# Opening of a four-layer kernel: loads in pieces in the order of use, scratch rows zeroed later

## The chip, the cores and the metric

The kernel runs on one core of one Trainium2 chip. Its time is the device time of one execution in microseconds; the median of several executions counts, and a change is measured by the ratio of the medians.

## The reference

x is (8, 256, 256), the context (8, 256, 192), the mask (8, 256) with one flag for each context row. Four layers follow one another, each a cross attention or a similarity and then a feed-forward part; LayerNorm stands before each.

```python
x = x + L0_xattn(layernorm(x), ctx, mask, ...)   # masked cross attention, 16 heads of 16
x = x + L0_ffn(layernorm(x), ...)                # top-1 experts, rows scattered to slots
x = x + L1_xattn(layernorm(x), ctx, ...)         # cosine similarity
x = x + L1_ffn(layernorm(x), ...)                # local transformer
x = x + L2_xattn(layernorm(x), ctx, ...)         # cross attention with biases and a scale
x = x + L2_ffn(layernorm(x), ...)                # top-2 experts
x = x + L3_xattn(layernorm(x), ctx, ...)         # cross attention, output bias
x = x + L3_ffn(layernorm(x), ...)                # grouped experts

def L0_xattn(x, context, context_mask, Wq, Wk, Wv, Wo):
    q, k, v = heads(x @ Wq), heads(context @ Wk), heads(context @ Wv)
    scores = einsum('bhid,bhjd->bhij', q, k) * 16 ** -0.5
    scores = where(context_mask[:, None, None, :], scores, -finfo.max)
    return merge(einsum('bhij,bhjd->bhid', softmax(scores), v)) @ Wo
```

## The kernel before

Five engines run their own instruction streams and meet at semaphores: TensorE (PE), VectorE (DVE), ScalarE (ACT), GpSimd (POOL) and SyncE (SP), which issues most DMAs. The 2048 rows of x stay on the chip as 16 tiles of 128 rows (`c.x`), the context transposed (`c.ctxT`, two chunks of 128 partitions by 2048 columns). A phase is a block: all engines leave it together.

`load_phase` is the first block. SP issues the loads of x (2 MB), the context (2 MB) and the identity, then, when GpSimd has filled a tile with zeros, one store that zeroes all 5120 slot rows of the scratch `rows_in` (5 MB), and waits for the loads. VectorE raises 72 semaphores to their starting count, one instruction each (line 143).

`xattn_phase` is the cross attention of layers 0, 2 and 3 (the tags L0x, L2x and L3x). SP issues its weights, and for layer 0 the mask, all on one semaphore (lines 364 to 373). VectorE measures mean and variance of the first four tiles (`measure(0)`), GpSimd takes the power -0.5 of the variance (line 351), and VectorE then waits for all loads, turns the mask into two things (line 779 to 782: `anyk`, whether a sequence has any key, and `mbias`, one row of 2048 biases), scales wq, and goes to `normalise_rows(0)`. TensorE begins when every load is in and VectorE's steps are done:

```python
            pe.wait_ge(*loaded(16 * n_loads))
            pe.wait_ge(*mstep(MSTEPS))
            project_keys(0)
            turn_rows(0)
            project_queries(0)
```

`project_keys(b)` (line 452) multiplies the context of sequence b with wk. ACT and DVE split the result into a leading part and a rest (`lead_keys`, `rest_keys`, line 795 or 798); `turn_rows(b)` (line 442) waits for that rest and for the normalised rows and transposes them, and `project_queries(b)` follows. Keys and queries go through DRAM to be stacked in three parts: `send_keys`, `stack_keys`, `send_queries`, `stack_queries` on SP, an order written out by hand, each waiting for the one before to land. Then TensorE goes over 8 sequences of 16 heads: scores of the next sequence for its row maxima (taken by DVE, line 816), and scores of this one with the maxima put in as a row. The maxima make a round trip through DRAM on ACT's own queue (`send_maxima`, `top_queries`, lines 654 and 661), twice a sequence. In the loop over sequences SP sends the queries of b + 2 and the keys of b + 3.

In `dispatch_phase` of layer 0's experts GpSimd waits for the zeros and scatters rows into `rows_in` (line 1097).

## Time and profile before

| | |
|---|---|
| median of 3 runs | 2955.56 us (2951.53 to 2962.20) |
| the profiled execution | 2948.41 us, its span 2946.5 us |
| mean granted clock of TensorE | 0.879 |
| busy | PE 2322.9 us, DVE 1290.0, ACT 1063.6, POOL 616.9 |
| DMA over the whole run | 165.65 MB |

The span runs from the first to the last instruction. Times in the rows are microseconds from the span's start; a shape is partitions x elements; SPq, ACTq and the like are the queues of an engine, where issues and waits stand. "idle before" names what ended the idle time of the engine just before the instruction. The granted clock is 1.00 at 2.4 GHz and 0.50 at 1.2 GHz.

### The profile page before, as it was taken

The numbers are of one execution on the slowest core, as the hardware profiler recorded it, in microseconds if no ns is written. First come the engines' busy times: TensorE is split into PE (matmuls) and PEld (weight loads), VectorE is DVE, ScalarE is ACT, GpSimd is POOL, SyncE is SP. The second block draws the span as 40 slices with busy tenths as digits, with TensorE's granted clock in tenths as the row PEclk, the third lists the DMA queues.
The fourth block names the chain that finished last, engine by engine and source line by source line (L and its number), as shares of the span: only waits on it lengthen the run. The fifth ranks groups of instructions, "written<-read, shape, count | busy, mean of one in ns | idle before, by whom it ended". The sixth has DMA issues, their size and how long they took to land. (4 is left out here: it accounts for less than half of the span.)

```text
span 2946.5 us, 43378 instructions
## 1 busy us (share of the span) xinstructions
PE 2322.9 (79%) x13240; PEld 1675.6 (57%) x13241; DVE 1290.0 (44%) x2837; ACT 1063.6 (36%) x2491; POOL 616.9 (21%) x623
## 2 busy tenths in 40 slices
PE   2896298448799698889597897897999179838998
PEld 1564197224465474456375564467999156517887
DVE  3564200459665425956522564300000246465554
ACT  0464132214355422346531355213444035513332
POOL 0001200217521323722131000220000400023333
PEclk9798599669799798979797699898999569969999
DMA  6660332000000100000101672213220366200001
GB/s 197 116 119 12 128 130 87 27 26 0 10 0 3 44 1 26 0 10 0 47 1 35 116 123 37 77 53 125 79 110 18 88 119 123 43 13 27 22 21 34
DMA packets 119273, 165.65 MB, mean 56 GB/s; under 512 B 14394, under 2 KB 106269, under 8 KB 114045
## 3 DMA queue, kind: packets, MB, share of 16 engines
q1 hardware_dynamic: 113236, 150.64, 20.5%
q0 software_dynamic: 4608, 12.59, 1.3%
q10 hardware_dynamic: 1320, 1.03, 0.2%
q8 instruction: 61, 1.00, 0.2%
q14 instruction: 48, 0.39, 0.0%
HBM read 114.43 MB, written 47.32 MB: 55 GB/s over the span
## 5 line engine op out<-in xcount | busy, mean ns | idle before, releaser
L816 DVE TENSOR_REDUCE xa_mx<-ps 128x2 f32<-128x512 f32 x384 | 256.9, 690 | 221.3 <-PE ps L478 213.0
L668 ACT ACTIVATE xn_tok<-ps 128x512 f32<-128x512 f32 x384 | 227.4, 602 | 168.0 <-PE ps L486 166.4
L478 PE MATMUL ps<-xa_ks,xa_qs 48*128 48x256 f32 (+1 forms) x768 | 182.5, 349 | 47.6 <-DVE xa_mx L816 21.0
L1315 PE MATMUL ps<-ex_tiles,ex_w 128*128 x1792 | 213.2, 278 | 7.7 <-issue 4.2
L1315 PEld LDWEIGHTS ps<-ex_tiles,ex_w 128*128 128x128 f32 x1792 | 212.6, 195 | 11.3 <-issue 8.5
L1321 PE MATMUL ps<-ex_w,ex_h 128*128 128x256 f32 x896 | 202.7, 379 | 0.0
L478 PEld LDWEIGHTS ps<-xa_ks,xa_qs 48*128 48x128 f32 (+1 forms) x768 | 118.5, 208 | 137.5 <-issue 80.9
L1835 PE MATMUL ps<-lp_wqkv,lp_hs 128*128 128x512 f32 x384 | 176.4, 611 | 4.6 <-ACT lp_hs L1879 4.3
L1321 PEld LDWEIGHTS ps<-ex_w,ex_h 128*128 128x128 f32 x896 | 166.0, 190 | 20.2
L486 PE MATMUL ps<-xa_qs,xa_ks 49*128 49x256 f32 (+1 forms) x768 | 173.3, 332 | 0.7 <-ACT xn_tok L668 0.7
L1335 ACT ACTIVATE ex_h<-ps,ex_b 128x128 f32<-128x128 f32 x296 | 108.8, 368 | 152.8 <-PE ps L1315 132.7
L452 PE MATMUL ps<-ctx_T,xa_wk 128*128 128x256 f32 x192 | 59.7, 464 | 128.4 <-DVE xa_wq L789 102.9
L255 PE MATMUL ps<-ident,ln_row 128*128 128x128 f32 x192 | 46.9, 399 | 122.9 <-DVE ln_row L225 121.5
L1373 POOL DMA_INDIRECT xn_tok<-rows_out,rows_back x32 | 31.5, 984 | 530.7 <-DMA rows_out<-ex_tiles 521.5
L1351 DVE TENSOR_TENSOR ex_tiles<-ps,ex_b 128x256 f32 x37 | 15.7, 425 | 276.6 <-PE ps L1321 270.0
L232 POOL TENSOR_TENSOR ln_rstd<-ln_var,pow_half 128x16 f32<-128x16 f32 x7 | 20.4, 2913 | 497.7 <-DVE ln_var L214 497.7
L1835 PEld LDWEIGHTS ps<-lp_wqkv,lp_hs 128*128 128x128 f32 x384 | 72.2, 194 | 90.1 <-issue 85.3
L1622 POOL TENSOR_TENSOR ge_hl<-ge_h,ge_hh 128x512 fp32r<-128x512 f32 x64 | 82.6, 1291 | 195.0 <-ACT ge_hh L1611 195.0
L452 PEld LDWEIGHTS ps<-ctx_T,xa_wk 128*128 128x128 f32 x192 | 41.9, 230 | 140.7 <-DMA xa_bo<-in_L3x_bo_dram 59.9
L486 PEld LDWEIGHTS ps<-xa_qs,xa_ks 49*128 49x128 f32 (+1 forms) x768 | 111.3, 195 | 9.3 <-ACT xn_tok L668 6.8
L1533 PE MATMUL ps<-ge_xh,ge_wh 128*128 128x512 f32 x256 | 81.8, 401 | 40.7 <-PEq L1400 24.5
L2085 ACT ACTIVATE lw_p<-ps,lw_nm 128x128 f32<-128x128 f32 (+1 forms) x256 | 106.3, 425 | 14.6 <-DVE lw_nm L2136 14.6
...
## 6 DMA issues: line engine op xcount, KB each, us to landing
...
x_keys<-xa_khl SPq DMA_DIRECT2D x24, 512.0 KB, 5.9
x_queries<-xa_qhl SPq DMA_DIRECT2D x24, 512.0 KB, 2.9
di_rows<-rows_in SPq DMA_DIRECT2D x16, 512.0 KB, 3.8
...
```

What stands on the lines that cost most here:

```text
L452: ins = nc.tensor.matmul(c.ps[:, W_BANK, ch * S:(ch + 1) * S], wk[:, k, ch * P:(ch + 1) * P], c.ctxT[:, k, b * S:(b + 1) * S], start=(k == ...
L478: ins = nc.tensor.matmul(c.ps[:, M_BANK + h % 2, qt * S:(qt + 1) * S], qs[r:r + ROWS_M, b % Q_BUFS, n, qt * P:(qt + 1) * P], ks[r:r + ROWS ...
L486: ins = nc.tensor.matmul(c.ps[:, S_BANK + (HEADS * b + n) % 3, kt * S:(kt + 1) * S], ks[r:r + ROWS_S, b % K_BUFS, h // 2, kt * P:(kt + 1) ...
L668: nc.scalar.activation(pT[:, h % SLOTS].rearrange("p k q -> p (k q)"), c.ps[:, S_BANK + (HEADS * b + n) % 3], ACT.Exp).then_inc(exped.sem, 1)
L816: nc.vector.tensor_reduce(mx[:, half, :, col], c.ps[:, M_BANK + h % 2].rearrange("p (t n) -> p t n", t=2), AX_X, ALU.max).then_inc(max_put ...
L1315: ins = nc.tensor.matmul(c.ps[:, f % 4, 0:P], w1[:, par, k, f * P:(f + 1) * P], tile_of(n)[:, k], start=(k == 0), stop=(k == KD - 1))
L1321: ins = nc.tensor.matmul(c.ps[:, 4, 0:D], h[:, f], w2[:, par, f], start=(f == 0), stop=(f == FC - 1))
L1335: nc.scalar.activation(h[:, f], c.ps[:, f % 4, 0:P], ACT.Relu if first else ACT.Silu, bias=0.0 if first else b1[:, par, f:f + 1]).then_inc ...
L1533: ins = nc.tensor.matmul(c.ps[:, 2 * (g % 2) + m, :], wp[:, par, at:at + I3], xp[:, k, cols], start=(a == 0 and k == 0), stop=(a == 2 and ...
L1622: nc.gpsimd.tensor_tensor(hl[:, g % 2], h[:, g % 2], hh[:, g % 2].bitcast(F32), ALU.subtract).then_inc(h_rest.sem, 1)
L1835: ins = nc.tensor.matmul(c.ps[:, 3 * tt + n, :], hs[:, k, tt * P:(tt + 1) * P], wqkv[:, k, n * INNER:(n + 1) * INNER], start=(k == 0), sto ...
L2085: ins = nc.scalar.activation(pr[:, h % AHEAD, lo:hi], c.ps[:, 1 + h % AHEAD, lo:hi], ACT.Exp, bias=nm[:, h, n:n + 1], accum_out=rs[:, h, n ...
```

## The change

The first block loses its loads, the store of zeros and the wait for them; what is left of it is raising the semaphores, now dealt to VectorE, TensorE, ScalarE and GpSimd (three names more), and GpSimd's four small memsets. The attention block issues, for layer 0: wk, the mask, the first 512 columns of the context, the first four tiles of x, the identity, wq, the other tiles of x, wv, the rest of the context, wo. Each has a semaphore of its own except wv and wo. TensorE begins with wk and the first context part; it waits for the scaled wq only ahead of `project_queries(0)`, and for wv and wo at head 4 of the first pass. The two mask operations that make `mbias` go from VectorE to GpSimd, ahead of its power steps, and read the bytes of one partition; `anyk` stays on VectorE, straight from the bytes. wq is scaled after `normalise_rows(0)` instead of before it. SP waits for `mbias` after `send_keys(0)`. The zeros are stored in eight pieces of 640 KB, one at the end of each turn of SP's loop over sequences; GpSimd's wait ahead of the scatter counts all eight. Layers 2 and 3 get the same waits, in the order wk, wq (with its scale), wv, wo, bo. `CTX_PARTS` is ((0, 512), (512, 2048)), `GROUPS` ((0, 4), (4, 16)); `mask_in`, `ctx_in`, `x_in`, `ident_in`, `kw_in` and `qw_in` are the new DMA semaphores, `any_key`, `rows_masked` and `scaled` the new ones of the engines.

```diff
@@ -134,33 +134,34 @@
 
 def load_phase(c):
 
-    nc, loaded, set_up = c.nc, c.sig("loaded"), c.sig("set_up")
+    nc, set_up = c.nc, c.sig("set_up")
     with nc.Block() as block:
+        def raise_signals(eng, quarter):
+            for name in SIGNALS[quarter::4]:
+                if name != "set_up":
+                    eng.sem_inc(c.sig(name).sem, START)
+
         @block.vector
         def _(dve):
-            for name in SIGNALS:
-                if name != "set_up":
-                    dve.sem_inc(c.sig(name).sem, START)
-
-        @block.sync
-        def _(sp):
-            for name, dst in (("x", c.x), ("ctxT", c.ctxT), ("ident", c.ident)):
-                sp.dma_start(dst[:], c.dram[name]).then_inc(loaded.sem, 16)
-
-            sp.wait_ge(*set_up(4))
-            rows = c.dram["rows_in"][0:SLOT_ROWS].rearrange("(a p) d -> p a d", p=P)
-            sp.dma_start(rows, c.zero[:].to_broadcast([P, SLOT_ROWS // P, D])).then_inc(c.sig("scratch_zeroed").sem, 16)
-            sp.wait_ge(*loaded(48))
+            raise_signals(dve, 0)
+
+        @block.tensor
+        def _(pe):
+            raise_signals(pe, 1)
+
+        @block.scalar
+        def _(act):
+            raise_signals(act, 2)
 
         @block.gpsimd
         def _(pool):
+            raise_signals(pool, 3)
             nc.gpsimd.memset(c.ones[:], 1.0).then_inc(set_up.sem, 1)
             nc.gpsimd.memset(c.half[:, 0], 0.5).then_inc(set_up.sem, 1)
             nc.gpsimd.memset(c.half[:, 1], -0.5).then_inc(set_up.sem, 1)
             nc.gpsimd.memset(c.zero[:], 0.0).then_inc(set_up.sem, 1)
             pool.sem_inc(set_up.sem, START)
             pool.wait_ge(*set_up(4))
-    loaded.spent(48)
     set_up.spent(4)
 
 
...
@@ -346,6 +351,14 @@
             nc.gpsimd.memset(consts[:, 0], -1.0).then_inc(consts_set.sem, 1)
             nc.gpsimd.memset(mx[:], 0.0)
             nc.gpsimd.memset(va[:], 1.0).then_inc(mstep.sem, 1)
+            if masked:
+                pool.wait_ge(*mask_in(16))
+                nc.gpsimd.tensor_scalar(mask[:], mask8[0:1], -1.0, HUGE, ALU.add, ALU.mult).then_inc(rows_masked.sem, 1)
+                pool.wait_ge(*rows_masked(1))
+                pool.wait_ge(*any_key(1))
+                nc.gpsimd.tensor_tensor(
+                    mbias[:].rearrange("p (b s) -> p b s", b=B), mask[:].rearrange("p (b s) -> p b s", b=B),
+                    anyk[0:1].unsqueeze(2).to_broadcast([1, B, S]), ALU.mult).then_inc(rows_masked.sem, 1)
             for n, (lo, hi) in enumerate(GROUPS):
                 pool.wait_ge(*variance(n + 1))
                 nc.gpsimd.tensor_tensor(rstd[:, lo:hi], var[:, lo:hi], c.half[:, 1, lo:hi], ALU.pow
...
@@ -359,18 +372,33 @@
                 pool.wait_ge(*bias_added(B))
             pool.wait_ge(*powered(len(GROUPS)))
             pool.wait_ge(*mstep(1))
+            if masked:
+                pool.wait_ge(*rows_masked(2))
 
         @block.sync
         def _(sp):
-            for dst, name in ((wk, "wk"), (wq, "wq"), (wv, "wv"), (wo, "wo")):
-                sp.dma_start(dst[:], dram[tag + name]).then_inc(loaded.sem, 16)
+            sp.dma_start(wk[:], dram[tag + "wk"]).then_inc(kw_in.sem, 16)
+            if masked:
+                sp.dma_start(mask8[:], dram["mask"].partition_broadcast(P)).then_inc(mask_in.sem, 16)
+                lo, hi = CTX_PARTS[0]
+                sp.dma_start(c.ctxT[:, :, lo:hi], dram["ctxT"][:, :, lo:hi]).then_inc(ctx_in[0].sem, 16)
+                lo, hi = GROUPS[0]
+                sp.dma_start(c.x[:, lo:hi], dram["x"][:, lo:hi]).then_inc(x_in[0].sem, 16)
+                sp.dma_start(c.ident[:], dram["ident"]).then_inc(ident_in.sem, 16)
+            sp.dma_start(wq[:], dram[tag + "wq"]).then_inc(qw_in.sem, 16)
+            if scale_in:
+                sp.dma_start(qcol[:], dram[tag + "qcol"]).then_inc(qw_in.sem, 16)
+                sp.dma_start(qscale[:], dram[tag + "scale"].partition_broadcast(P)).then_inc(qw_in.sem, 16)
+            if masked:
+                lo, hi = GROUPS[1]
+                sp.dma_start(c.x[:, lo:hi], dram["x"][:, lo:hi]).then_inc(x_in[1].sem, 16)
+            sp.dma_start(wv[:], dram[tag + "wv"]).then_inc(loaded.sem, 16)
+            if masked:
+                lo, hi = CTX_PARTS[1]
+                sp.dma_start(c.ctxT[:, :, lo:hi], dram["ctxT"][:, :, lo:hi]).then_inc(ctx_in[1].sem, 16)
+            sp.dma_start(wo[:], dram[tag + "wo"]).then_inc(loaded.sem, 16)
             if biased:
                 sp.dma_start(bo[:], dram[tag + "bo"].partition_broadcast(P)).then_inc(loaded.sem, 16)
-            if scale_in:
-                sp.dma_start(qcol[:], dram[tag + "qcol"]).then_inc(loaded.sem, 16)
-                sp.dma_start(qscale[:], dram[tag + "scale"].partition_broadcast(P)).then_inc(loaded.sem, 16)
-            if masked:
-                sp.dma_start(mask8[:], dram["mask"].partition_broadcast(P)).then_inc(loaded.sem, 16)
 
             def send_keys(b):
                 sp.wait_ge(*k_rest(b + 1))
...
@@ -421,6 +449,9 @@
             stack_queries(1)
             send_keys(2)
             stack_keys(2)
+            if masked:
+                clear = SLOT_ROWS // P // B
+                rows = dram["rows_in"][0:SLOT_ROWS].rearrange("(a p) d -> p a d", p=P)
             for b in range(B):
                 if b + 2 < B:
                     send_queries(b + 2)
...
@@ -428,10 +459,15 @@
                 if b + 3 < B:
                     send_keys(b + 3)
                     stack_keys(b + 3)
+                if masked:
+                    sp.dma_start(rows[:, b * clear:(b + 1) * clear], c.zero[:].to_broadcast([P, clear, D])
+                                 ).then_inc(c.sig("scratch_zeroed").sem, 16)
 
         @block.tensor
         def _(pe):
             def turn_rows(b):
+                if masked and b == 0:
+                    pe.wait_ge(*ident_in(16))
                 pe.wait_ge(*normed(b + 1))
                 if b < 3:
                     pe.wait_ge(*k_rest(b + 1))
...
@@ -447,6 +483,8 @@
                 pe.wait_ge(*q_rest(b))
                 if b == 2:
                     pe.wait_ge(*v_put(1))
+                    if masked:
+                        pe.wait_ge(*ctx_in[1](16))
                 for ch in range(KD):
                     for k in range(KD):
                         ins = nc.tensor.matmul(c.ps[:, W_BANK, ch * S:(ch + 1) * S], wk[:, k, ch * P:(ch + 1) * P],
...
@@ -556,10 +594,12 @@
                                                wo[:, k], start=(k == 0), stop=(k == KD - 1))
                 ins.then_inc(y_done.sem, 1)
 
-            pe.wait_ge(*loaded(16 * n_loads))
-            pe.wait_ge(*mstep(MSTEPS))
+            pe.wait_ge(*kw_in(16))
+            if masked:
+                pe.wait_ge(*ctx_in[0](16))
             project_keys(0)
             turn_rows(0)
+            pe.wait_ge(*scaled(SCALES))
             project_queries(0)
             project_keys(1)
             turn_rows(1)
...
@@ -568,6 +608,7 @@
             for n in range(HEADS):
                 step(-1, n)
                 if n == 4:
+                    pe.wait_ge(*loaded(16 * n_loads))
                     project_values(0)
                 elif n == HALF:
                     turn_maxima(0, 0)
...
@@ -687,7 +728,9 @@
                 if masked:
                     act.dma_start(qs[at - 1:at].bitcast(F32).rearrange("p n g s -> p (n g) s"),
                                   consts[:, 1:2].to_broadcast([1, Q_BUFS * PAIRS, S])).then_inc(rows_set.sem, 16)
-            act.wait_ge(*mstep(MSTEPS))
+            act.wait_ge(*mstep(1))
+            if masked:
+                act.wait_ge(*any_key(1))
             lead_keys(0)
             put_rows(0)
             lead_queries(0)
...
@@ -744,6 +787,8 @@
 
             def measure(n):
                 lo, hi = GROUPS[n]
+                if masked:
+                    dve.wait_ge(*x_in[n](16))
                 for t in range(lo, hi):
                     ins = nc.vector.bn_stats(stats[:, t].rearrange("p a b -> p (a b)"), c.x[:, t])
                 chain.link(dve, ins)
...
@@ -770,24 +815,20 @@
                                                   rstd[:, n:n + 1], ALU.subtract, ALU.mult)
                 ins.then_inc(normed.sem, 1)
 
+            if masked:
+                dve.wait_ge(*mask_in(16))
+                nc.vector.tensor_reduce(anyk[:], mask8[:].rearrange("p (b s) -> p b s", b=B), AX_X, ALU.max
+                                        ).then_inc(any_key.sem, 1)
+            dve.wait_ge(*mstep(1))
             measure(0)
-            step = Steps(mstep)
-            step.n = 1
-            dve.wait_ge(*mstep(1))
-            dve.wait_ge(*loaded(16 * n_loads))
-            if masked:
-                step.link(dve, nc.vector.tensor_copy(mask[:], mask8[:]))
-                step.link(dve, nc.vector.tensor_reduce(anyk[:], mask[:].rearrange("p (b s) -> p b s", b=B), AX_X, ALU.max))
-                step.link(dve, nc.vector.tensor_scalar(mask[0:1], mask[0:1], -1.0, HUGE, ALU.add, ALU.mult))
-                step.link(dve, nc.vector.tensor_tensor(
-                    mbias[:].rearrange("p (b s) -> p b s", b=B), mask[0:1].rearrange("p (b s) -> p b s", b=B),
-                    anyk[0:1].unsqueeze(2).to_broadcast([1, B, S]), ALU.mult))
-            if scale_in:
-                step.mark(nc.vector.tensor_scalar(qcol[:], qcol[:], qscale[:, 0:1], None, ALU.mult))
-                step.link(dve, nc.vector.tensor_scalar(wq[:], wq[:], qscale[:, 0:1], None, ALU.mult))
-            else:
-                step.link(dve, nc.vector.tensor_scalar(wq[:], wq[:], scale, None, ALU.mult))
-            assert step.n == MSTEPS
+
+            def scale_queries():
+                dve.wait_ge(*qw_in(16 * n_query_loads))
+                if scale_in:
+                    nc.vector.tensor_scalar(qcol[:], qcol[:], qscale[:, 0:1], None, ALU.mult).then_inc(scaled.sem, 1)
+                    nc.vector.tensor_scalar(wq[:], wq[:], qscale[:, 0:1], None, ALU.mult).then_inc(scaled.sem, 1)
+                else:
+                    nc.vector.tensor_scalar(wq[:], wq[:], scale, None, ALU.mult).then_inc(scaled.sem, 1)
 
             def rest_keys(b):
                 dve.wait_ge(*k_put(b + 1))
...
@@ -836,6 +877,7 @@
                 nc.vector.tensor_tensor(xb, xb, c.ps[:, Y_BANK], ALU.add).then_inc(y_added.sem, 1)
 
             normalise_rows(0)
+            scale_queries()
             rest_keys(0)
             normalise_rows(1)
             rest_queries(0)
...
@@ -1091,7 +1141,7 @@
 
         @block.gpsimd
         def _(pool):
-            pool.wait_ge(*zeroed(16))
+            pool.wait_ge(*zeroed(16 * B))
             for t in range(NT):
                 for n in range(top):
                     nc.gpsimd.indirect_dma_start(c.dram["rows_in"], bass.IndirectOffsetOnAxis(slots[:, n, t:t + 1], 0),
```

## Rows read from the trace of the kernel before

**Rows 1.** Stretches: us, busy us of each engine, then granted clock, DMA share, GB/s
```profile
5.00:15.40 10.40, 0.00 (x0) 0.00 (x0) 0.00 (x0) 0.00 (x0) 0.00 (x0) 1.00 0.99 380
27.00:32.00 5.00, 0.00 (x0) 0.00 (x0) 0.00 (x0) 0.00 (x0) 0.00 (x0) 1.00 0.82 254
32.00:43.40 11.40, 0.00 (x0) 0.00 (x0) 7.45 (x6) 0.00 (x0) 0.00 (x0) 1.00 0.09 28
43.40:99.00 55.60, 38.95 (x123) 26.86 (x124) 24.50 (x52) 10.35 (x17) 2.27 (x1) 0.66 0.65 119
150.00:200.00 50.00, 47.77 (x408) 31.93 (x407) 32.50 (x57) 29.68 (x61) 0.00 (x0) 1.00 0.67 127
```

**Rows 2.** Timeline, opening: start us, us, engine, line, operation, count [idle before <-releaser]
```profile
15.42 11.40 SPq L366 DMA_DIRECT2D xa_wk<-in_L0x_wk_dram  x1
15.46 1.41 DVE L748 BATCH_NORM_STATS2 xa_stats<-x_res 128x6 f32<-128x256 f32 x4 [15.34 <-PEq L138]
...
16.38 1.80 POOL L348 MEMSET xa_v<- 128x2048 f32 x1
...
17.17 1.04 DVE L752 TENSOR_SCALAR xa_mean<-xa_total 128x4 f32<-128x4 f32 x1
...
19.29 1.02 POOL L351 TENSOR_TENSOR xa_rstd<-xa_var,pow_half 128x4 f32<-128x4 f32 x1 [1.11 <-DVE xa_var L760]
...
35.77 1.23 DVE L779 CAST xa_mask<-xa_mask 128x2048 f32<-128x2048 uint8 x1 [16.56 <-DMA xa_mask<-in_mask_dram]
37.03 2.29 DVE L780 TENSOR_REDUCE xa_anyk<-xa_mask 128x8 f32<-128x2048 f32 x1
...
42.92 0.43 DVE L789 TENSOR_SCALAR xa_wq<-xa_wq 128x512 f32<-128x512 f32 x1
43.38 0.73 DVE L769 TENSOR_SCALAR xa_row<-x_res,xa_mean,xa_rstd 128x256 f32<-128x256 f32 x2
...
43.45 3.75 PE L452 MATMUL ps<-ctx_T,xa_wk 128*128 128x256 f32 x8 [43.45 <-DVE xa_wq L789]
...
49.29 0.75 DVE L795 SCALAR_TENSOR_TENSOR xa_khl<-ps,xa_anyk,xa_khl 128x512 fp32r<-128x512 f32 x1 [5.17 <-ACT xa_khl L626]
...
50.19 0.63 PE L442 MATMUL ps<-ident,xa_row 128*128 128x128 f32 x4 [2.99 <-DVE xa_khl L795]
```

**Rows 3.** Line 143: count, ns min/median/max, first and last start us
```profile
L143 DVEq EVENT_SEMAPHORE  x72: 21/21/21, 0.8 to 7.8; - x72
```

**Rows 4.** DMA issues, first 60 us: count, KB each, us to landing
```profile
rows_in<-zero SPq DMA_DIRECT2D x1, 5120.0 KB, 30.4
...
x_keys<-xa_khl SPq DMA_DIRECT2D x1, 512.0 KB, 2.9
```

**Rows 5.** GpSimd's groups by shape: count | busy us, mean ns | idle
```profile
L1622 POOL TENSOR_TENSOR ge_hl<-ge_h,ge_hh 128x512 fp32r<-128x512 f32 x64 | 82.6, 1291 | 195.0 <-ACT ge_hh L1611 195.0
...
L1445 POOL TENSOR_TENSOR ge_xl<-xn_T,ge_xh 128x1024 fp32r<-128x1024 f32 x4 | 12.8, 3217 | 27.3 <-ACT ge_xh L1436 27.3
```

**Rows 6.** Timeline, opening of layer 3
```profile
2341.03 0.35 SPq L366 DMA_DIRECT2D xa_wk<-in_L3x_wk_dram  x1
...
2347.98 0.43 DVE L789 TENSOR_SCALAR xa_wq<-xa_wq 128x512 f32<-128x512 f32 x1 [3.41 <-DMA xa_bo<-in_L3x_bo_dram]
...
2352.83 0.69 DVE L798 TENSOR_TENSOR xa_khl<-ps,xa_khl 128x512 fp32r<-128x512 f32 x1 [3.65 <-ACT xa_khl L628]
```

**Rows 7.** Timeline, opening of layer 2, VectorE
```profile
1605.43 0.23 DVE L786 TENSOR_SCALAR xa_qcol<-xa_qcol,xa_qscale 128x2 f32<-128x2 f32 x1 [3.83 <-DMA xa_qscale<-in_L2x_scale_dram]
...
1610.61 0.69 DVE L798 TENSOR_TENSOR xa_khl<-ps,xa_khl 128x512 fp32r<-128x512 f32 x1 [3.79 <-ACT xa_khl L628]
```

**Rows 8.** Timeline of SyncE in the steady part
```profile
142.71 0.66 SPq L397 DMA_DIRECT2D xa_ks<-xa_mbias  x1
149.34 0.38 SPq L382 DMA_DIRECT2D x_queries<-xa_qhl  x1
```

**Rows 9.** Timeline of ScalarE in the steady part
```profile
147.10 0.59 ACT L638 CAST xa_qhl<-ps 128x512 fp32r<-128x512 f32 x1 [2.14 <-DMA x_maxima<-xa_mxT]
```

28 lines of the change are left out of this document (20 added, 8 removed).

## The prediction

> **What bounds the kernel now.** I read the stretches first. From 5 to 43.4 us the program does almost nothing but load: TensorE has no instruction. Up to 15.4 us 380 GB/s move, from 27 to 32 us 254, and from 32 to 43.4 us the DMA engines are idle (share 0.09) while VectorE works alone on the mask. From 150 us on TensorE is busy 47.8 of 50 us at full clock: there it sets the pace, and what is saved ahead of it moves everything behind it forward by as much [rows 1].
>
> Then the chain of starts in the opening. The first block ends when its last load has landed; the attention block's first load is issued at 15.42 us, and that one issue takes 11.40 us, because SyncE pushes it in behind the 5 MB of zeros. VectorE stands 16.56 us until the last load of the block, the mask, is in at 35.8; it makes the mask rows in four linked steps (the two shown are 1.23 and 2.29 us), scales wq, and only then the PE begins: 43.45. Keys take 3.75 us, ACT and DVE split them, and the first transpose of x starts at 50.19 [rows 2]. That instruction is my mark: before it the order of work changes, behind it in this layer nothing does but the zeroing.
>
> **When the new opening issues its first load.** The first block has no load left. Raising 72 semaphores took VectorE from 0.8 to 7.8 us, 99 ns each [rows 3]. The changed kernel has 75 of them and deals them to four engines, 19 on GpSimd: 1.9 us. The four small memsets behind them I put at 1 us (all four are far smaller than the one of 1.80 us [rows 2]); with the start and the barrier, SyncE issues wk at about 3.8 us, against 15.42.
>
> **When the pieces land.** 512 KB stored with nothing else in the queues landed 2.9 us after issue [rows 4]. wk and the mask are 512 KB, the mask is issued some 0.4 us later: in at 7.2. The first quarter of the context is 512 KB in pieces of 2 KB; at the 254 GB/s of the stretch in which the weights (2 KB a partition too) came in [rows 1] it needs 2.0 us: 9.2. x's first four tiles follow at a rate between 254 and 380: 10.7. All loads together, 5.4 MB, end near 20 us, just as the first keys are sent to DRAM; nothing of the 5 MB of zeros is in front any more.
>
> **What then sets the mark.** Two paths. PE: keys from 9.2 to 13.0; from their end to VectorE's step on them it was 2.1 before (47.20 to 49.29), so 15.1. VectorE: its `rest_keys(0)`, which releases the mark, now stands behind `normalise_rows(0)` and `scale_queries`, so behind the power step on GpSimd, and GpSimd has the two mask operations in front of its power step. GpSimd has no such operation in this trace. The first, one input and 2048 elements on one partition: not below the memset of as many elements, 1.80 [rows 2], not above a two-input one, 5.2; I take 2.6, near the memset: 7.2 to 9.8. VectorE's reduction over the mask (2.29) is done by 9.5 and costs nothing. The second has two inputs: 1.291 us for 512 elements, 3.217 for 1024 [rows 5], so 5.2 to 6.4 for 2048; I take 5.2, the rate of the shorter: 15.0. Meanwhile VectorE measures x. Its third step there, 4 elements wide, took 1.04 us before and ended at 18.21, when the memset on GpSimd ended (16.38 + 1.80 = 18.18) [rows 2]: it will sit again until GpSimd is through, 15.1, and from there to the power step it is 1.1 (18.21 to 19.29): 16.2. Power step 1.0: 17.2. Normalise 0.8, scale wq 0.4, `rest_keys(0)` 0.8: **19.2**. Before, that instruction ended at 49.29 + 0.75 = 50.04 [rows 2]. Gain 30.8 us.
>
> The Trainium skill, "SBUF — State Buffer", section "SBUF: two separate sides", says that the port pair which VectorE and GpSimd share is locked for a whole instruction and the other engine stands still. The row of 1.04 us agrees. By that rule, handing the mask rows to GpSimd beside a measuring VectorE is dear; by the row the gain is 30.8, and without a lock it would be 31.8, since the power step is queued behind the mask rows in any case.
>
> Bounds of this term: a first mask operation of 5.2 and a second of 6.4 cost 3.8 more, a landing 2 us later another 2: gain 25. Mask rows that hide altogether leave the measuring: 10.7 + 3.8 (15.46 to 19.29) + 1.0 + 2.0 = 17.5, gain 32.5.
>
> **Layers 2 and 3.** There TensorE waited for all loads and for the scaled wq; now for wk alone. Layer 3: wk is issued at 2341.03, VectorE was done measuring at 2347.98 - 3.41 = 2344.57, wq was scaled only at 2347.98 because bo landed then, and `rest_keys(0)` ended at 2353.52 [rows 6]. New: wk, half of the 512 KB that took 2.9, in after 2.4; keys 3.75 to 2347.2; ACT 0.65; rest 0.7: 2348.5. VectorE is ready at 2344.57 + 1.1 + 0.8 + 0.4 = 2346.9, not in the way. Gain 5.0 (4.5 if wk takes the whole 2.9). Layer 2: VectorE ended at 1605.43 - 3.83 = 1601.60, so the block began at about 1598.05, and `rest_keys(0)` ended at 1611.30 [rows 7]. New: wk in at 1600.5, keys to 1604.2, rest to 1605.5, gain 5.8; if wq and its scale land no earlier than 1605.43, the two scalings (0.7) and the rest (0.7) end at 1606.8, gain 4.5. I take 5.5. Together 10.5 (9.0 to 10.8).
>
> **The zeroed rows.** Eight stores of 640 KB in place of one of 5120 KB that took 30.4 us in the opening [rows 4]; at 380 GB/s [rows 1] 1.7 us each. SyncE ends the stack of keys at 143.37 and has nothing to send until 149.34 [rows 8]: a gap of 6.0 us in each sequence, and the piece is issued at its head, so the next queries find the queue empty. What it can meet is ScalarE's own round trip of the maxima, which ScalarE waits for already (2.14 us there [rows 9]). At worst every piece adds its 1.7: 13.4. At best nothing: TensorE has work for that long. The share of DMA goes from 0.67 to about 0.75 in that stretch. I take 1. The scatter that waits for the zeros starts hundreds of microseconds later. The other edits (a wait for the identity, for the second part of the context and of x, for wv at head 4) name loads that are in by 20 us and cost nothing; were the loads 5 us late, the measuring of the other twelve tiles would be the first to feel it.
>
> **Sum.** 30.8 + 5.5 + 5.0 - 1 = 40.3 us. The profiled execution took 2948.4, so it would be 2908.1; the median of the runs is 7.1 above that execution, so I give 2955.6 - 40.3 = **2915**. A measurement of this kernel can tell 0.3%, 9 us, from no change.
>
> **Rivals.**
> *The zeros collide.* Each of the eight pieces stands in front of a maxima round trip and ScalarE, then TensorE, lose its whole length: 13.4 instead of 1, 2928. For it: ScalarE's wait of 2.14 shows that the trip is exposed. Against it: these are a few KB on ScalarE's own queue, and TensorE is busy 47.8 of 50 us in that part [rows 1]. 0.10.
> *GpSimd is the new neck.* The mask rows at their upper price and late pieces: opening gains 25, 2921. For it: GpSimd is the only engine with three steps in a line there. 0.17.
> *The clock moves.* Between 43.4 and 99 us the granted clock is 0.66 on the mean, between its two levels, 1.2 and 2.4 GHz [rows 1]. TensorE's idle time before its first work and between keys and transposes changes (now 6 us, from 13.0 to 19.2, before 3), and the half-speed stretch may grow or shrink. If it grows by a third of its some 30 us, 5 to 8 us are lost: 2922; if it shrinks as much, 2908. 0.10 and 0.10.
> *Nothing gained.* If the load of x and context were hidden by other work, moving it would be worth nothing, 2955. The stretches to 43.4 show no TensorE work at all to hide it. 0.03.
> *Slower.* The pieces of zeros hold up the stacks of keys and queries, TensorE waits at the head of each of eight sequences. It decides from 41.3 / 8 = 5.2 us a sequence; a piece of 1.7 us in a gap of 6.0 does not reach it. If each cost a whole gap beyond the first, 6.0 + 1.7 = 7.7, the time were 2955.6 - 41.3 + 61.6 = 2976. 0.03.
> The forecast itself (2910 to 2919) has 0.47.
>
> **Range and chances.** One bound at a time: the opening's upper gain, 32.5 + 10.8, is 43.3 (2912); its lower one 25 + 10.5 - 1 = 34.5 (2921); the zeros' bound 30.8 + 10.5 - 13.4 = 27.9 (2928). With the clock's 5 to 8 either way and the spread of the runs shown (4.0 below the median, 6.6 above): 2902 to 2932. It leaves out the last two rivals and two bad bounds together, under 2 in 10. Faster by over 0.3%: 0.94, within: 0.03, slower: 0.03.
>
> **What the changed profile would show.** SyncE issues wk near 3.8 us in under 1 us, not 11.4; the first TensorE matmul near 9.2; the mask operations on GpSimd between 7 and 15, with the short step of measuring on VectorE stretched to their end; the transpose of x at 19 to 20; in layers 2 and 3 the PE's first matmul 2.5 us behind the issue of wk; stores of zeros in the gaps from 90 us on, and the steady stretch as busy as before (47.8 of 50). I would be wrong if the measuring waited for x (pieces much slower than 254 GB/s), if the power step came after 22 us, or if TensorE's share fell in the steady stretch.

## Result and the profile after

The changed kernel took 2933.13 us (median of 4 runs, 2930.40 to 2938.74) against 2953.77 (4 runs) of the kernel before: a ratio of 0.9927 [0.9902, 0.9953]. Two later comparisons of the same two kernels gave 0.9896 [0.9868, 0.9924] and 0.9886 [0.9866, 0.9905]. So it is faster, as forecast; 2933 is 18 us above the 2915 and 1 us above the range. The three savings were 20.6, 32.6 and 34.3 us, all below the forecast 40.3.

The head of the page of the changed kernel; its profiled execution took 2930.4 us:

```profile
span 2928.6 us, 43391 instructions
...
PE 2340.0 (80%) x13240; PEld 1686.4 (58%) x13241; DVE 1282.3 (44%) x2834; ACT 1062.3 (36%) x2491; POOL 621.5 (21%) x625
```

The busy times are within 1% of those of before, TensorE's even 17 us longer (2340.0 against 2322.9), so the 17.9 us between the spans were gained in waiting, not in work. Stretches of the changed kernel, columns as in [rows 1]:

```profile
4.00:15.00 11.00, 3.49 (x8) 2.53 (x8) 3.93 (x8) 0.00 (x0) 8.20 (x6) 1.00 0.89 253
15.00:27.00 12.00, 5.92 (x15) 3.98 (x15) 4.05 (x13) 3.14 (x4) 1.02 (x1) 1.00 0.81 308
27.00:42.30 15.30, 6.89 (x19) 4.39 (x18) 6.61 (x22) 1.86 (x3) 2.27 (x1) 0.82 0.93 153
42.30:99.00 56.70, 47.62 (x286) 31.94 (x287) 31.20 (x52) 20.51 (x41) 0.00 (x0) 0.75 0.70 124
130.00:180.00 50.00, 47.14 (x418) 31.39 (x422) 33.18 (x57) 30.37 (x63) 0.00 (x0) 1.00 0.76 147
193.00:201.00 8.00, 5.70 (x52) 3.82 (x54) 4.20 (x7) 4.04 (x8) 0.00 (x0) 0.98 1.10 284
201.00:224.00 23.00, 22.09 (x125) 13.41 (x126) 8.88 (x16) 8.98 (x19) 0.00 (x0) 0.56 0.02 6
```

The empty first 43 us of [rows 1] are gone. The steady stretch, 130 to 180 us, is as busy as before (47.1 against 47.8 of 50), with pieces of zeros inside it, and the DMA share rose from 0.67 to 0.76, as forecast. The last two lines are new. From 193 to 201 us the queues are full and TensorE works 5.7 of 8 us; behind that it runs at a clock of 0.56.

The opening in the timeline of the changed kernel, against [rows 2]:

```profile
3.97 0.38 SPq L380 DMA_DIRECT2D xa_wk<-in_L0x_wk_dram  x1
...
8.74 1.89 POOL L356 TENSOR_SCALAR xa_mask<-xa_mask 1x2048 f32<-1x2048 uint8 x1 [2.02 <-DMA xa_mask<-in_mask_dram]
11.12 3.59 POOL L359 TENSOR_TENSOR xa_mbias<-xa_mask,xa_anyk 1x2048 fp32r<-1x2048 f32 x1 [0.49 <-DVE xa_anyk L820]
...
11.51 3.75 PE L490 MATMUL ps<-ctx_T,xa_wk 128*128 128x256 f32 x8 [11.51 <-DMA ctx_T<-in_ctxT_dram]
13.28 1.41 DVE L793 BATCH_NORM_STATS2 xa_stats<-x_res 128x6 f32<-128x256 f32 x4 [2.32 <-DMA x_res<-in_x_dram]
...
14.99 0.17 DVE L797 TENSOR_SCALAR xa_mean<-xa_total 128x4 f32<-128x4 f32 x1
...
16.23 1.02 POOL L364 TENSOR_TENSOR xa_rstd<-xa_var,pow_half 128x4 f32<-128x4 f32 x1 [1.52 <-DVE xa_var L805]
...
18.28 0.75 DVE L836 SCALAR_TENSOR_TENSOR xa_khl<-ps,xa_anyk,xa_khl 128x512 fp32r<-128x512 f32 x1
...
19.17 1.09 PE L478 MATMUL ps<-ident,xa_row 128*128 128x128 f32 x4 [3.91 <-DVE xa_khl L836]
...
42.39 0.80 PE L516 MATMUL ps<-xa_ks,xa_qs 49*128 49x256 f32 x4 [6.17 <-DMA xa_qs<-x_queries]
```

The mark, the first transpose, moved from 50.19 to 19.17: a gain of 31.0 us, forecast 30.8. (In the other two profiles of the changed kernel it stands at 19.93 and 19.66.) But the first scores moved only 27.5, from 69.86 in the timeline of the kernel before to 42.39:

```profile
69.86 0.80 PE L478 MATMUL ps<-xa_ks,xa_qs 49*128 49x256 f32 x4 [4.78 <-DMA xa_qs<-x_queries]
```

One more place in this trace, around 190 us, was not forecast. SyncE's timeline, then TensorE's:

```profile
158.63 0.44 SPq L463 DMA_DIRECT2D rows_in<-zero  x1
...
189.80 2.84 SPq L437 DMA_DIRECT2D xa_qs<-x_queries  x6
192.68 2.31 SPq L463 DMA_DIRECT2D rows_in<-zero  x3
...
199.56 0.35 PE L516 MATMUL ps<-xa_ks,xa_qs 49*128 49x256 f32 x1 [2.15 <-DMA xa_qs<-x_maxima]
```

Pieces 1 to 5 go one at a time; pieces 6, 7 and 8 are issued together, behind the last stack of queries, because the sixth turn of SyncE's loop has no keys to send behind its queries, and the last two turns have nothing to wait for at all. The reload of the maxima, two transfers of 4 KB that ScalarE issues at 193.46, releases TensorE only at 199.56; TensorE has run out of work at 197.4, and its clock stands at the half level for 20.5 us from 200.7 on. The three profiles of the changed kernel have this wait (2.15, 2.27 and 2.27 us; the half-speed stretch behind it is 10.2 us long in the other two). Both of the kernel before have 0.7 us at this place, the pause that stands at the same place of the earlier sequences too. A gap of 2.5 to 3.5 us some 44 us behind the first scores is in the kernel before too and no part of the change.

To have one number of the first attention I take the start of its last addition to x, in each kernel. One addition closes each of the eight sequences, and the fifth and the sixth show where the time goes. First the kernel before, then the changed one:

```profile
225.69 0.68 DVE L836 TENSOR_TENSOR x_res<-x_res,ps 128x512 f32<-128x512 f32 x1
...
244.94 0.68 DVE L836 TENSOR_TENSOR x_res<-x_res,ps 128x512 f32<-128x512 f32 x1
...
273.04 0.69 DVE L836 TENSOR_TENSOR x_res<-x_res,ps 128x512 f32<-128x512 f32 x1 [4.97 <-PE ps L555]
```

```profile
196.38 0.68 DVE L877 TENSOR_TENSOR x_res<-x_res,ps 128x512 f32<-128x512 f32 x1
...
224.92 0.68 DVE L877 TENSOR_TENSOR x_res<-x_res,ps 128x512 f32<-128x512 f32 x1
...
254.62 0.69 DVE L877 TENSOR_TENSOR x_res<-x_res,ps 128x512 f32<-128x512 f32 x1 [5.66 <-PE ps L593]
```

The gain in this pair is 29.3 us at the fifth addition, 20.0 at the sixth and 18.4 at the last. From the fifth to the sixth, where the burst lies, the kernel before takes 19.25 us and the changed one 28.54. My theory A was that the burst of three pieces holds up the maxima, costs TensorE the gap and then the clock, some 7 us together. Theory B was that the clock alone, which differs between executions in this part too, makes that difference, with no help from the zeros.

### The profile page after: what moved, and what is told of

Read it like the earlier page. It is cut to its first block and busy times, and to the rows that moved or that the text cites. A ratio compares the mean times of both kernels' runs of the same rounds, so it can differ in the third digit from the quotient of the medians.

```text
span 2928.6 us, 43391 instructions
## 1 busy us (share of the span) xinstructions
PE 2340.0 (80%) x13240; PEld 1686.4 (58%) x13241; DVE 1282.3 (44%) x2834; ACT 1062.3 (36%) x2491; POOL 621.5 (21%) x625
## 3 DMA queue, kind: packets, MB, share of 16 engines
q1 hardware_dynamic: 113892, 150.64, 20.8%
## 5 line engine op out<-in xcount | busy, mean ns | idle before, releaser
L1365 PEld LDWEIGHTS ps<-ex_tiles,ex_w 128*128 128x128 f32 x1792 | 211.8, 194 | 10.8 <-issue 8.1
L1371 PEld LDWEIGHTS ps<-ex_w,ex_h 128*128 128x128 f32 x896 | 166.3, 191 | 19.9
L1583 PE MATMUL ps<-ge_xh,ge_wh 128*128 128x512 f32 x256 | 81.9, 402 | 40.7 <-PEq L1450 24.4
L564 PE MATMUL ps<-xn_tok,xa_v 128*32 128x256 f32 x1536 | 108.0, 401 | 5.6 <-ACT xn_tok L709 5.6
```

The lines of the kernel that those rows point to most:

```text
L564: ins = nc.tensor.matmul(c.ps[j * SLOT:(j + 1) * SLOT, O_BANK, 0:S], va[:, b % 2, kt, h], pT[:, h % SLOTS, kt], start=(kt == 0), stop=(kt ...
L1365: ins = nc.tensor.matmul(c.ps[:, f % 4, 0:P], w1[:, par, k, f * P:(f + 1) * P], tile_of(n)[:, k], start=(k == 0), stop=(k == KD - 1))
L1371: ins = nc.tensor.matmul(c.ps[:, 4, 0:D], h[:, f], w2[:, par, f], start=(f == 0), stop=(f == FC - 1))
L1583: ins = nc.tensor.matmul(c.ps[:, 2 * (g % 2) + m, :], wp[:, par, at:at + I3], xp[:, k, cols], start=(a == 0 and k == 0), stop=(a == 2 and ...
```

## Experiments

**The burst taken away, in three ways.** All against the changed kernel. `three_last` keeps five pieces in the loop and issues the last three when the last maxima are in:

```diff
-                if masked:
+                if masked and b < 5:
                     sp.dma_start(rows[:, b * clear:(b + 1) * clear], ...)
...
+            if masked:
+                sp.wait_ge(*max_in[1](32 * B))
+                for b in range(5, B):
+                    sp.dma_start(rows[:, b * clear:(b + 1) * clear], ...)
```

> The changed kernel with only the last three of the eight pieces of zeros moved: they are stored once the last round trip of the maxima is over instead of three in a row at 192.7 us. Theory A (the burst of three pieces stands in front of the sequence's maxima, TensorE idles 2.15 us at 197.4 us and its clock falls to half for 20.5 us): the idle gap and the half-speed stretch at 200.7 us are gone, 7 to 9 us faster than the changed kernel, near 2925. Theory B (the clock falls there of itself, by where its windows lie): the gap goes, the half-speed stretch stays or sits elsewhere, within 3 us of the changed kernel.

Measured: 2921.35 us, 0.9881 [0.9836, 0.9927] of the kernel before (2963.11 in this comparison). Its stretches behind the old place of the burst, and its last addition:

```profile
193.00:201.00 8.00, 7.26 (x63) 4.78 (x65) 4.55 (x7) 4.63 (x10) 0.00 (x0) 1.00 0.56 68
201.00:224.00 23.00, 20.08 (x177) 12.34 (x178) 11.09 (x20) 13.47 (x29) 0.00 (x0) 0.93 0.01 3
```

```profile
246.50 0.69 DVE L882 TENSOR_TENSOR x_res<-x_res,ps 128x512 f32<-128x512 f32 x1 [5.11 <-PE ps L598]
```

The gap is down to the usual 0.7 us, and of the half-speed stretch 3.4 us are left, at 208.8, with no longer gap ahead of them. The attention ends 8.1 us earlier than in the changed kernel.

`zeros_last` issues all eight pieces there, none in the loop:

```diff
-                if masked:
+            if masked:
+                sp.wait_ge(*max_in[1](32 * B))
+                for b in range(B):
                     sp.dma_start(rows[:, b * clear:(b + 1) * clear], ...)
```

> The changed kernel with all eight pieces of zeros stored after the last round trip of the maxima, so that none meets the attention. Theory A: the same as with three moved, near 2925, since the five single pieces met a gap. If the single pieces cost too (the rival of the prediction in which each piece costs its length, 1.7 us), another 5 to 8 us faster, near 2918. Theory B: near 2933.

Measured: 2920.47 us, 0.9870 [0.9829, 0.9912]; last addition at 246.47, the same as with five pieces in the loop (246.50). That equality is partly luck: the fifth addition comes 3.2 us later (200.64 against 197.45), and the rest is quicker. The better sign is the time from the first addition to the fifth, in which pieces 2 to 5 are stored. It is 87.6 to 87.7 us in 15 of the 18 profiles, with the pieces (all three of the changed kernel) and without them (both of the kernel before). The three others are `burst_early`, below, and `zeros_last` (89.2) and `best_again` (91.5), in both of which the clock fell there. Single pieces cost nothing that shows there.

`no_burst` moves the same 5 MB in five pieces of 1 MB, one in each of the first five turns:

```diff
-                clear = SLOT_ROWS // P // B
+                clear = SLOT_ROWS // P // 5
...
-                if masked:
+                if masked and b < 5:
```

> The same zeros in five pieces of 1 MB, one in each of the first five turns, none behind them. Theory A: no gap in the sixth and seventh sequence, near 2925, unless 2.7 us of stores in a gap of 6 us begin to delay the queries. Theory B: near 2933.

Measured: 2924.70 us, 0.9884 [0.9841, 0.9926]; no wait of TensorE for a DMA behind 100 us, last addition at 245.97. So it is not the sum of the megabytes. What is left is how much of them goes at once, or at which place of the turn: the burst is issued behind a stack of queries, every single piece behind a stack of keys. No kernel here sends one piece alone at the place of the burst.

**The burst put elsewhere.** `burst_early` sends pieces 3 to 6 together in the third turn, where keys and queries still come behind them, and has no burst at the end:

```diff
+                    for n in ((0,), (1,), (2, 3, 4, 5), (6,), (7,), (), (), ())[b]:
+                        sp.dma_start(rows[:, n * clear:(n + 1) * clear], ...)
```

> The changed kernel with the burst put elsewhere: the third turn of SyncE's loop stores four pieces of zeros in a row (at about 136 us), the fourth and fifth one each, the last three none. Theory A (a burst in front of the maxima stops TensorE): the gap in TensorE's work and a wait for the maxima of some 2 us or more move to 137 to 145 us, and none is left near 197 us. Whether a half-speed stretch follows the gap there is the second question; if it does, the first attention ends as late as in the changed kernel. Rival (the last sequences are slow for a reason of their own): the gap near 197 us stays.

Measured: 2948.12 us, 0.9901 [0.9872, 0.9929]. SyncE and TensorE in its timeline:

```profile
140.03 3.66 SPq L464 DMA_DIRECT2D rows_in<-zero  x4
...
160.51 0.45 PE L517 MATMUL ps<-xa_ks,xa_qs 49*128 49x256 f32 x1 [1.71 <-DMA xa_qs<-x_maxima]
```

The long wait at the end is gone (0.78 us at 206.6, as in every kernel without a burst there), so the last sequences have no reason of their own. A wait of 1.71 us comes at 160.5, and not between 137 and 145 as I expected. The burst held up the store of the queries behind it, issued at 146.09: 6.4 us to landing in place of 3.3. So their stack was issued from 152.53 to 155.23, and the reload of the maxima at 154.85; the changed kernel has 2.9 us between the two. That this meeting made the wait is argued, not shown. The attention ended at 255.44, about as late as with the burst at the end, but only a part of that is the burst's. Against the usual distance of the additions, 3.5 us were lost between the first and the second, before the burst was issued, 4.6 between the second and the fourth, and 2.6 between the fifth and the sixth. Each loss has a half-speed stretch of 6.8 us in it, at 112.8, 160.6 and 208.4.

**One store in the opening.** `one_store` has the new loads, but all zeros in one store, issued behind wo:

```diff
             sp.dma_start(wo[:], dram[tag + "wo"]).then_inc(loaded.sem, 16)
+            if masked:
+                rows = dram["rows_in"][0:SLOT_ROWS].rearrange("(a p) d -> p a d", p=P)
+                sp.dma_start(rows, c.zero[:].to_broadcast([P, SLOT_ROWS // P, D])
+                             ).then_inc(c.sig("scratch_zeroed").sem, 16)
```

> The opening of the changed kernel, but the zeros in one store of 5 MB right behind the last weights, as the kernel before had it in its first block. About 14 us of stores are then queued from about 18 us on, in front of the first keys and queries. If the order of the transfers matters, the first scores (42.4 us in the changed kernel) start 10 to 14 us later, and the kernel takes 2933 + 10 - 8 (no burst), near 2935. If the zeros were harmless, near 2925.

Measured: 2931.69 us, 0.9903 [0.9876, 0.9930]. SyncE and TensorE in its timeline:

```profile
19.93 12.87 SPq L409 DMA_DIRECT2D x_keys<-xa_khl  x1
...
56.30 0.80 PE L514 MATMUL ps<-xa_ks,xa_qs 49*128 49x256 f32 x4 [10.19 <-DMA xa_qs<-x_queries]
```

The long issue is back, now on the first keys: 12.87 us, as 11.40 on wk in [rows 2]. The first scores come 13.9 us later than in the changed kernel, the fifth addition 13.2 us later (209.62). With no burst the way to the sixth is 9.3 us shorter. Another 3.2 us are made up behind it, where the changed kernel's clock was at the half level for 10.2 us from 245.1 on and this one's was not. So the last addition comes only 0.8 us later (255.45).

**Layers 2 and 3.** `old_waits_23` gives these two layers their old order of waits back:

```diff
             if masked:
                 pe.wait_ge(*ctx_in[0](16))
+            else:
+                pe.wait_ge(*loaded(16 * n_loads))
+                pe.wait_ge(*scaled(SCALES))
             project_keys(0)
...
+            if not masked:
+                dve.wait_ge(*loaded(16 * n_loads))
+                scale_queries()
             normalise_rows(0)
```

> The changed kernel with the waits of layers 2 and 3 undone: there TensorE and the scaling of wq wait for all loads again, layer 0 stays as changed. If the early start is worth what the marks show (5 us in each), this kernel is 10 us slower than the changed one, near 2943, and keys of layer 2 and 3 start 5 us later after their block begins. If it is lost again behind them (the rival), it is as fast as the changed kernel.

Measured: 2953.75 us, 0.9906 [0.9870, 0.9942], where the changed kernel had 0.9896 in the same comparison. It is 7.9 us slower, where 10 were expected, and the intervals overlap: too little for the time to tell. The trace can. From the issue of wk to the end of the keys' rest the kernel before takes 13.24 us in layer 2 and 12.49 in layer 3, this one 12.79 and 12.23, the changed one 8.42 and 8.27. Behind it the gain is mostly kept: from the issue of wk to the attention's last addition the kernel before takes 239.7 and 237.2 us (mean of two profiles), the changed one 235.4 and 233.6 (mean of three), though its profiles differ by up to 5 us and this kernel's 237.2 and 234.7 lie between. Layer 2 of the changed kernel:

```profile
1590.42 0.35 SPq L380 DMA_DIRECT2D xa_wk<-in_L2x_wk_dram  x1
...
1592.97 1.41 DVE L793 BATCH_NORM_STATS2 xa_stats<-x_res 128x6 f32<-128x256 f32 x4 [2.90 <-POOL xa_v L353]
1593.19 3.74 PE L490 MATMUL ps<-ctx_T,xa_wk 128*128 128x256 f32 x8 [8.03 <-DMA xa_wk<-in_L2x_wk_dram]
...
1598.16 0.68 DVE L839 TENSOR_TENSOR xa_khl<-ps,xa_khl 128x512 fp32r<-128x512 f32 x1
```

TensorE begins 2.8 us behind the issue of wk (forecast 2.4 to 2.5). VectorE begins to measure only when GpSimd's memset is done; the diff moved its wait for `mstep` ahead of `measure(0)`, which I had read over.

**Two small repairs.** `late_loads` is `three_last` with wv, the second part of the context and wo issued behind the first stack of queries:

```diff
+            def late_loads():
+                sp.dma_start(wv[:], ...)
+                sp.dma_start(c.ctxT[:, :, lo:hi], ...)
+                sp.dma_start(wo[:], ...)
...
             stack_queries(0)
+            if masked:
+                late_loads()
```

> The three last pieces of zeros stored behind the maxima, and in layer 0 wv, the second part of the context and wo loaded after the first queries' stack instead of before the first keys. In the changed kernel the first keys, sent at 19.05 us, landed only at 24.8, in 5.7 us where the kernel before took 2.9, and the first queries, ready at 26.12, were sent at 29.84. Theory C (2 MB of late loads stood in front of the keys and SyncE's order handed the delay on): the keys land 2.9 us after they are sent, the queries follow within 1 us of being ready, first scores 2.5 to 3 us earlier than in the kernel with only the three pieces moved, and the whole 3 us faster. Rival: the 3 us are lost by the half-speed clock in the projections, and the first scores stay within 0.5 us.

Measured: 2943.14 us, 0.9892 [0.9858, 0.9925]. The keys' store lands in 2.9 us again in place of 5.2 in `three_last` and 5.7 in the changed kernel, and the first scores start at 40.49, 2.1 us earlier than in `three_last`. But TensorE then waits 0.9 us at 45.31 for the loads that were put off, and the last addition (248.14) is not earlier. The 3 us expected of the whole did not come.

`best` is `late_loads` with the measuring ahead of the wait for the memsets:

```diff
-            dve.wait_ge(*mstep(1))
             measure(0)
+            dve.wait_ge(*mstep(1))
```

> Both repairs together (three pieces behind the maxima, late loads behind the first queries' stack) and in all three attentions VectorE's wait for GpSimd's memset of 2048 elements put behind the first measuring, where the kernel before had it. In the changed kernel VectorE idled 2.90 us for that memset at the start of layers 2 and 3. If that wait counts, keys' rest in layers 2 and 3 is done 0.4 to 0.6 us earlier (then TensorE's path, wk in at 2.7 and keys of 3.8, is the longer one), not 2.9. The whole 10 to 14 us faster than the changed kernel, a ratio to the kernel before near 0.985.

Measured: 2941.41 us, 0.9899 [0.9860, 0.9938], and in a second comparison 2946.77, 0.9876 [0.9837, 0.9915]. Layer 2 of `best`:

```profile
1579.38 0.34 SPq L380 DMA_DIRECT2D xa_wk<-in_L2x_wk_dram  x1
1579.43 1.41 DVE L804 BATCH_NORM_STATS2 xa_stats<-x_res 128x6 f32<-128x256 f32 x4 [0.40 <-PEq L2261]
1581.14 0.78 DVE L808 TENSOR_SCALAR xa_mean<-xa_total 128x4 f32<-128x4 f32 x1
...
1586.69 0.69 DVE L850 TENSOR_TENSOR xa_khl<-ps,xa_khl 128x512 fp32r<-128x512 f32 x1 [1.20 <-ACT xa_khl L680]
```

VectorE starts 2.5 us earlier after the issue of wk, and the keys' rest ends 8.00 us after it in place of 8.42: TensorE's path is nearly as long, so the early measuring gives 0.4. The ratio near 0.985 that I expected did not come.

**The mask rows on VectorE.** `mask_on_dve` is `three_last` with both mask operations on VectorE, ahead of the measuring:

```diff
+                nc.vector.tensor_scalar(mask[:], mask8[0:1], -1.0, HUGE, ALU.add, ALU.mult)...
+                nc.vector.tensor_tensor(mbias[:]..., mask[:]..., anyk[0:1]..., ALU.mult)...
             dve.wait_ge(*mstep(1))
             measure(0)
```

> The three last pieces of zeros stored behind the maxima, and the two mask operations back on VectorE, between the reduction of the mask and the measuring. In the changed kernel GpSimd was through with them at 14.71 us, before the variance at 16.16, so they cost nothing there. On VectorE they take 1.2 + 2.3 us behind the reduction (to some 14.5 us), past the landing of x at 13.3: the first transpose of x starts 1 to 1.5 us later. If GpSimd's lock or its queue was the neck after all (a rival of the prediction), it starts earlier instead.

Measured: 2947.21 us, 0.9902 [0.9870, 0.9935]. The first transpose starts at 20.29, in `three_last` at 20.08, in the changed kernel at 19.17. The two operations take 1.20 and 2.28 us on VectorE in place of 1.89 and 3.59, but they stand in front of its measuring, which begins at 14.42 in place of 13.28. But the kernels with the changed opening differ among themselves by more: 19.17 to 21.32 us in twelve profiles. So neither order wins by anything that shows here; the last addition (243.16) is as early as the earliest of `three_last` (243.21).

**The same kernels again.** To get the burst and the clock apart, the kernel before, the changed one, `three_last`, `zeros_last` were profiled and timed again.

> The kernel before, for its trace alone. If the long half-speed stretch in the local attention is a matter of windows, the kernel before can show it as well, in its first or its second layer; if only the changed opening causes it, 37.5 and 34.1 us again.

Measured: one execution, 2987.47 us, span 2985.2; last addition at 274.68.

> The changed kernel once more, beside the others on one chip. Two questions. Size of the burst's cost: 7 to 9 us slower than the kernel with three pieces moved, by theory A. And the half-speed stretch in the first local attention of layer 1 (61.4 us from 750 us on in the changed kernel, 34 to 38 us in the kernel before and in two of the four variants): if it is a matter of where the clock's windows lie and not of the code, a second execution of the same code may show 35 to 38 us there, and the time of that stretch varies by some 9 us from run to run. If the change causes it, it shows 61 again.

Measured: 2945.89 us, 0.9896 [0.9868, 0.9924]; last addition at 252.52. The half-speed stretch in layer 1 is 61.4 us again.

```profile
199.31 0.68 DVE L877 TENSOR_TENSOR x_res<-x_res,ps 128x512 f32<-128x512 f32 x1
...
223.74 0.68 DVE L877 TENSOR_TENSOR x_res<-x_res,ps 128x512 f32<-128x512 f32 x1
```

> The kernel with the last three pieces of zeros moved behind the maxima, a second time, on the same chip as the changed kernel. Theory A: no half-speed stretch between 190 and 225 us and 7 to 9 us faster than the changed kernel. The other theory (the clock falls by itself): the same time as the changed kernel within 3 us.

Measured: 2937.12 us, 0.9860 [0.9825, 0.9894]; last addition at 247.39.

```profile
199.32 0.68 DVE L882 TENSOR_TENSOR x_res<-x_res,ps 128x512 f32<-128x512 f32 x1
...
218.61 0.68 DVE L882 TENSOR_TENSOR x_res<-x_res,ps 128x512 f32<-128x512 f32 x1
```

Up to the fifth addition this pair is alike to 0.01 us, at the sixth it is 5.1 us apart.

> The changed kernel a third time, beside the three repaired ones on one chip. Theory A: slower than the kernel with three pieces moved by 5 to 10 us (what the end of the first attention showed on two chips), with TensorE idle for about 2 us near 197 us. If the two are within 3 us of each other, the burst costs trace time that other parts give back.

Measured: 2945.39 us, 0.9886 [0.9866, 0.9905]; last addition at 250.67.

> Three pieces of zeros behind the maxima, third time: ratio to the kernel before 0.985 to 0.989, 5 to 10 us below the changed kernel on the same chip.

Measured: 2939.53 us, 0.9865 [0.9841, 0.9889]; last addition at 243.21.

> All eight pieces behind the maxima, second time. Within 3 us of the kernel with three pieces moved, if single pieces in the gaps of a sequence are free as predicted; 5 us faster or more if each costs.

Measured: 2942.11 us, 0.9869 [0.9847, 0.9892]; last addition at 246.18.

> Three pieces moved, late loads and early measuring, second time. By the marks it should be 2 us (late loads) and 0.8 us (measuring, twice 0.4) below the kernel with three pieces moved; the first time the pair could not be told apart across calls. If it is not below it here either, the two small repairs are lost in what follows.

Measured as told above, and not below `three_last` (2939.53 in the same comparison); last addition at 245.06 (244.47 the first time). This profile, of a kernel without a burst, has a wait for the maxima at the head of the third sequence, with no zeros stored beside it (the piece before went out at 90.13), and 6.8 us at half speed behind it:

```profile
110.28 0.35 PE L527 MATMUL ps<-xa_ks,xa_qs 49*128 49x256 f32 x1 [1.46 <-DMA xa_qs<-x_maxima]
```

The last addition on the mean: before 273.9 (2 profiles), changed 252.6 (3), `three_last` 245.7 (3), `zeros_last` 246.3 (2). At the last addition the burst costs 8.1, 5.1 and 7.5 us in the three pairs, 6.9 on the mean; in time, medians of the same comparison, 8.8 and 5.9, where the intervals of the two kernels overlap. The sharper measure is the way from the fifth addition to the sixth: 28.5, 24.4 and 24.3 us in the changed kernel and 26.4 in `old_waits_23`, which has the burst too, against 19.3 in eleven of the thirteen profiles without a burst in or ahead of the stretch, the kernel before included, and 20.8 in the other two. That is 5 to 9 us.

Theory A holds for this stretch: the four profiles with a burst at the end have a wait of 1.9 to 2.3 us before the seventh sequence, and none of the fourteen others has more than 0.8 there. But a wait for the maxima with a fall of the clock behind it does not need a burst, as `best_again` shows, and the clock falls for 3.4 us without a longer wait between 190 and 210 us in three of the profiles without one (`three_last`, `zeros_last`, `best`).

Theory B holds elsewhere. From 700 to 830 us, in the local attention of layer 1, nothing is changed. The kernel before and the same kernel once more:

```profile
700.00:830.00 130.00, 106.84 (x411) 58.20 (x411) 96.73 (x184) 52.18 (x140) 68.00 (x74) 0.86 0.02 6
```

```profile
700.00:830.00 130.00, 106.85 (x356) 56.90 (x355) 91.14 (x157) 48.24 (x121) 67.48 (x72) 0.77 0.02 6
```

One kernel, a granted clock of 0.86 or 0.77, half-speed stretches of 37.5 or 61.4 us; between two of ScalarE's instructions there it took 11.6 us the first time and 20.8 the second, and over the 85 us behind ScalarE's table load at 782.2 us the second profile needs 10.7 us more. The first profile of the changed kernel has the 20.8, `three_last` 11.7, `zeros_last` 20.8. So one and the same kernel can lie either way. It is not shown that the change has no part in it: all three profiles of the changed kernel have the long stretch.

## Why the prediction was right in direction and too low

The profiled pair, cut at marks that both kernels have: 18.4 us gained up to the last addition of the first attention, 10.8 lost from there to the issue of wk in layer 2, 6.3 gained from there to wk of layer 3 and 4.0 from there to the end. Together that is the 17.9 by which the spans differ; forecast were 29.8, 0, 5.5 and 5.0. So of the 22.4 us that are missing here, 11.4 lie in the first attention (0.5 up to its fifth addition, 9.3 from there to the sixth, 1.6 behind it), 10.8 in a part in which nothing was changed (10.4 of them behind ScalarE's table load in layer 1, where the clock is at the half level), and 0.2 in layers 2 and 3.

**First load.** Forecast 3.8, measured 3.97. Right.

**Landings.** Forecast 7.2 (mask), 9.2 (context), 10.7 (x); measured about 8.7, 11.5 and 13.3. The rate from 4 to 15 us was 253 GB/s, what I had taken; the pieces came 1.5 to 2.6 us late. 512 KB stored alone took 2.9 us [rows 4]; the context's 512 KB took 6.5 us with its neighbours in the queues, x's 7.6. I had let the loads land one after another in the order of issue, but later loads took part of the rate: up to 11.5 us 1.5 MB had moved, and wk, the mask and the first context part are 1.0. VectorE did wait for x (2.32 us), which I had named as a sign of being wrong. The last part of the context landed at 22.8 us, where I had all loads in near 20.

**GpSimd.** Forecast 2.6 and 5.2 for the mask operations, measured 1.89 and 3.59. They were through at 14.71, not 15.0, and x came so late that the short step of measuring began at 14.99, behind them, and took 0.17 us: the lock that I had expected there (the Trainium skill, "SBUF — State Buffer", section "SBUF: two separate sides") never met it. Where the measuring does run beside the memset, in layer 2 of `best`, the same step takes 0.78 us and ends with the memset, which agrees with the rule. But not every instruction of VectorE is held up: the reduction of the mask (2.29 us) and the first step of measuring (1.41) ran beside GpSimd's two operations and took as long as without them (2.29 in [rows 2], 1.39 in `mask_on_dve`). Early GpSimd and late x cancelled in this profile: the power step started at 16.23, forecast 16.2, and the keys' rest ended at 19.03, forecast 19.2. Here the right number came from two wrong ones, and from an early execution: the twelve profiles with this opening have the mark at 19.9 us on the mean.

**Behind the mark.** I said that in this layer nothing changes behind it but the zeroing. 3.5 of the 31.0 us were lost before the first scores. The first keys were stored while the last loads were still moving (5.7 us to landing against 2.9). SyncE stacks them before it sends the queries, and so the first queries went out 10.7 us behind the mark in place of 7.2. Of that, 2.8 us are the keys' landing and 0.7 the issuing of the stacks (5.0 us in place of 4.4); the queries had been ready at 26.12. From the mark to the first scores it is 23.2, 22.2 and 21.9 us in the three profiles of the changed kernel, against 19.7 and 20.0 before. `late_loads` and `best` (20.8, 20.2, 20.2, against 22.5, 21.9 and 21.2 in `three_last`) show that the late loads are the cause of 1 to 2 us; in `late_loads` they were given away again 5 us later.

**The zeros: the step that failed.** I had written: "a gap of 6.0 us in each sequence, and the piece is issued at its head, so the next queries find the queue empty", and from it took 1 us for eight pieces. That holds for five of them. The gap is there only where a stack of keys ends the turn: behind the sixth turn's queries nothing is left to wait for, so three pieces go at once into the time of the maxima's reload. In the pair that the forecast is measured against it cost 9.3 us from the fifth addition to the sixth, 5.1 and 5.0 in the two others, 6.9 on the mean at the last addition: some 1.5 us of longer gap and the rest clock. The rival "the zeros collide" had the right victim, the maxima, but priced each piece at its 1.7 us; it was one burst that hurt, through its first consequence. The rival of the clock had the right effect with no cause named, and looked at the wrong place, 43 to 99 us.

**The clock elsewhere: a term put at nothing.** The forecast counts no change of the clock in parts that stay as they were, and its range gives the clock 5 to 8 us in the opening alone. The first pair lost 10.8 us in such a part. The half-speed stretch there is 61.4 us long in place of 37.5; why it is so long in this execution stays open.

With the burst taken away `three_last` measured 0.9881, 0.9860 and 0.9865, and 2915 of 2955.56 is 0.9863. The forecast of the time is then right, but its traces give 28.2 us at the last addition and not 29.8, so part of that agreement is luck.

**Layers 2 and 3.** Forecast 5.5 and 5.0, measured 4.8 and 4.2: wk took 2.8 us to land in place of 2.4, and the moved wait, missed in the diff, costs 0.4.

**The sum.** 31.0 - 3.5 at the first scores, 28.2 at the last addition without a burst, 21.3 with it, and 9.0 in layers 2 and 3, on the mean of the profiles: 30.3 us in place of 40.3, of which 6.9 are the burst, 1.6 the way from the first transpose to the last addition (29.8 forecast there, 28.2 measured), and 1.5 layers 2 and 3. The three measured savings, 20.6, 32.6 and 34.3, lie around it; the first, against which the forecast was made, is the lowest. Parts that are alike in code differ enough between executions to make such a difference: from wk of layer 2 to wk of layer 3 the three profiles of the changed kernel take 737, 760 and 757 us. That this explains the three savings is argued and not shown run by run.

**What beats both kernels** is `three_last`, or as good `zeros_last`: some 40 us faster than the kernel before (38 to 43 in five measurements). `late_loads` and `best` are not faster than they. From the changed kernel `three_last` is told apart by its traces; by the times alone the intervals overlap.
